# An attention layer with top-1 experts: gate and up weights as the stationary operand, row transposes ahead of up

## The chip, the cores and the metric

The kernel runs on one core of a Trainium2 chip. The metric is the device time of one execution in microseconds. Time before: 1159.86 us, the median of three runs (1158.37 to 1161.86).

## The reference

One transformer layer in fp32 on x of shape (4, 1024, 256). Causal attention with 16 heads of 16 and rotary embedding comes first, then a norm; then a feed-forward part with 8 experts, of which each token takes one:

```python
x = layernorm(x + attention(x))
xf = layernorm(x, ln_w, ln_b).reshape(-1, 256)
logits = xf @ router_w                       # 8 experts
top_idx, top_score = argmax(logits), sigmoid(max(logits))
for e in range(8):                           # gate_w, up_w: (8, 256, 512); down_w: (8, 512, 256)
    xe = xf * where(top_idx == e, top_score, 0)[:, None]
    routed += (silu(xe @ gate_w[e]) * (xe @ up_w[e])) @ down_w[e]
shared = (silu(xf @ sh_gate) * (xf @ sh_up)) @ sh_down
out = layernorm(x + (x + routed + shared))
```

## The kernel before, in words

Three programs run one after the other: `project` (queries, keys and values), `attend` (attention), and `feed` (everything behind it). Only `feed` is touched.

`feed` has two stages. In the first, 8 blocks of 512 tokens go through the output projection, two norms, the router and the shared expert. Each token's row (256 numbers, scaled by its score, and its token number behind them) is scattered by GpSimd to a table in HBM, `expert_rows`, at a place that its expert and its rank there give; the sum so far goes to `expert_sums`. Block 7, the last, runs side by side with the start of the second stage.

The second stage is one of 39 *slots* (`SLOTS`), written out, not looped by the chip. A slot j is 128 rows of one expert. Which expert it has is known at run time alone: VectorE writes it to `owner_i`, and an engine that needs it loads it into a register (`value_load`, L1027, L1038, L1046 on TensorE). A slot takes these steps:

- `load_rows(j)` on SyncE: loads the 128 rows into `rows[j % 3]`, a ring of three. `load_sums(j)` does so for the sums.
- `turn_rows(j)` on TensorE (L1020): two transposes into `front_ps`; `keep_rows(j)` on ScalarE (L1146) copies them to `rows_t`.
- `expert_gate(j)` (L1031) and `expert_up(j)` (L1041) on TensorE: two matmuls each. The rows, transposed, are the stationary operand; the weights, 512 columns at a time and addressed by the register, stream. The result has a token per partition.
- `make_silu` on ScalarE (L1133), `times_up` on VectorE (L1285): `hidden`, 128 tokens by 512.
- `turn_hidden(j)` on TensorE (L1003): four transposes; `keep_hidden(j)` on ScalarE (L1138) copies them to `hidden_t`.
- `expert_down(j)` on TensorE (L1051): four matmuls of 256 columns, into `down_ps` or, for odd slots, `front_ps`.
- `add_sum(j)` on VectorE: the sum of down's result and the loaded sum (L1367), then a CAST that takes the token numbers from the row buffer to `target_i` (L1369) and counts `targets_made`, then the moments (L1374, L1377). GpSimd makes the reciprocal deviation (L1478, L1483), VectorE's `normalise(j)` (L1382) uses it one slot later, and GpSimd scatters the result (L1491).

The order is written out by hand for each engine, and the engines meet at semaphores. TensorE's iteration j is gate(j+1), turn_hidden(j), up(j+1), turn_rows(j+2), down(j). VectorE's is times_up(j+1), normalise(j-1), add_sum(j). SyncE's is load_rows(j+3), load_sums(j+2), and for the load of rows the ring sets two waits, the rows that were in the buffer being turned and their token numbers being taken:

```python
if j >= ROW_RING:
    sp.wait_ge(rows_turned, j - ROW_RING + 1)
    sp.wait_ge(targets_made, j - ROW_RING + 1)
```

So load_rows(j+3) waits for the CAST of add_sum(j), which comes behind down(j). An fp32 matmul of the program shows as two in the trace, a transpose as one.

Of the kernel before, what the change touches and what calls it, by code (L numbers as in the profile page):

```python
# [28 lines left out]
P = 128  # L29
# [4 lines left out]
DC = D // P  # L34
# [713 lines left out]
def feed(nc, io, keep, scratch, out):  # L748
# [6 lines left out]
    with ExitStack() as ctx:  # L755
# [13 lines left out]
        row = b.sb("row", [P, 2, BT, RECORD])  # L769
        total = b.sb("total", [P, 2, BT, D])  # L770
        silu = b.sb("silu", [P, 2, INNER])
        hidden = b.sb("hidden", [P, 2, INNER])
        hidden_t = b.sb("hidden_t", [P, 2, INNER])
        shared_t = b.sb("shared_t", [P, IC, BLOCK])
        stats = b.sb("stats", [P, BT, 6])
# [79 lines left out]
        front_step = b.sem("front_step")  # L855
        gate_done, up_done, silu_made, hidden_made = (
            b.sem("gate_done"), b.sem("up_done"), b.sem("silu_made"), b.sem("hidden_made"))
        hidden_turned, hidden_t_kept, down_done, added = (
            b.sem("hidden_turned"), b.sem("hidden_t_kept"), b.sem("down_done"), b.sem("added"))
        block = ctx.enter_context(nc.Block())  # L860
        x_blocks = io["x"].rearrange("(n t p) d -> n p t d", t=BT, p=P)
        dve_stood, pool_stood = b.sem("dve_stood"), b.sem("pool_stood")
        VEC_STEPS = 16

        def slot_down(j):
            return front_ps[:, 1, :D] if j % 2 else down_ps[:]
# [61 lines left out]
        def _(pe):  # L928
# [67 lines left out]
                                            start=(c == 0), stop=(c == IC - 1))  # L996
                last.then_inc(down_done, 1)

            def turn_hidden(j):
                pe.wait_ge(hidden_made, TILES + j + 1)  # L1000
                wait(pe, hidden_t_kept, j)
                for c in range(IC):
                    last = nc.tensor.transpose(hidden_ps[:, c * P:(c + 1) * P],  # L1003
                                               hidden[:, j % 2, c * P:(c + 1) * P], ident[:])
                last.then_inc(hidden_turned, 1)

            def front_alone(n, batch, odd):
                for part in (turn_heads, times_wo, turn_xf, route, count_ranks):
                    part(n, batch, odd)
# [14 lines left out]
            def expert_gate(j):  # L1024
                if j >= SLOTS:
                    return
                e = pe.value_load(owner_i[0:1, j:j + 1], min_val=0, max_val=EXPERTS - 1)  # L1027
                pe.wait_ge(rows_t_kept, j + 1)
                pe.wait_ge(silu_made, TILES + j - 1)
                for c in range(DC):  # L1030
                    last = nc.tensor.matmul(gate_ps[:, j % 2], rows_t[:, j % 2, c * P:(c + 1) * P], gate_w[:, e, c],  # L1031
                                            start=(c == 0), stop=(c == DC - 1))
                last.then_inc(gate_done, 1)

            def expert_up(j):
                if j >= SLOTS:
                    return
                e = pe.value_load(owner_i[0:1, j:j + 1], min_val=0, max_val=EXPERTS - 1)  # L1038
                pe.wait_ge(hidden_made, TILES + j - 1)
                for c in range(DC):  # L1040
                    last = nc.tensor.matmul(up_ps[:, j % 2], rows_t[:, j % 2, c * P:(c + 1) * P], up_w[:, e, c],  # L1041
                                            start=(c == 0), stop=(c == DC - 1))
                last.then_inc(up_done, 1)

            def expert_down(j):
                e = pe.value_load(owner_i[0:1, j:j + 1], min_val=0, max_val=EXPERTS - 1)  # L1046
                pe.wait_ge(hidden_t_kept, j + 1)
                if j != 1:
                    pe.wait_ge(added, TILES + max(j - 1, 0))
                for c in range(IC):  # L1050
                    last = nc.tensor.matmul(slot_down(j), hidden_t[:, j % 2, c * P:(c + 1) * P], down_w[:, e, c],  # L1051
                                            start=(c == 0), stop=(c == IC - 1))
                last.then_inc(down_done, 1)
# [42 lines left out]
            by_batch(pe, step)  # L1096
            for j in range(SLOTS):
                expert_gate(j + 1)
                turn_hidden(j)
                expert_up(j + 1)  # L1100
                turn_rows(j + 2)
                expert_down(j)

        @block.scalar
        def _(act):
# [29 lines left out]
            def keep_hidden(j):  # L1135
                act.wait_ge(hidden_turned, j + 1)
                act.wait_ge(down_done, TILES + j - 1)
                nc.scalar.copy(hidden_t[:, j % 2], hidden_ps[:]).then_inc(hidden_t_kept, 1)  # L1138

            def keep_rows(j):  # L1140
                if j >= SLOTS:
# [6 lines left out]
            def block_step(i, odd, nxt, after):  # L1148
                def front(part):
                    if nxt is not None:  # L1150
                        part(i + 1, nxt, 1 - odd)

                for n in range(IC):
                    make_silu(i, n)
                if nxt is None:
                    keep_rows(0)
                    keep_rows(1)
                    make_silu(BLOCKS, 0)
                front(keep_xf)
# [15 lines left out]
            for j in range(SLOTS):  # L1175
                if j + 1 < SLOTS:
                    make_silu(BLOCKS, j + 1)
                keep_hidden(j)
                keep_rows(j + 2)

        @block.vector
        def _(dve):
# [93 lines left out]
            def times_up(i, t):  # L1276
                dve.wait_ge(silu_made, BT * i + t + 1)
                dve.wait_ge(up_done, BT * i + t + 1)
                if isinstance(i, int) and i == BLOCKS:
                    wait(dve, hidden_turned, t - 1)  # L1280
                    out = hidden[:, t % 2]
                else:
                    wait(dve, down_done, BT * i)
                    out = shared_t[:, t]
                nc.vector.tensor_tensor(out, silu[:, t % 2], up_ps[:, t % 2], ALU.mult).then_inc(hidden_made, 1)  # L1285

            def add_shared(i, t, odd, batch):
                dve.wait_ge(down_done, BT * i + t + 1)
                if t == 0:
                    wait(dve, sums_scattered[odd], 16 * BT * batch)  # L1290
                nc.vector.scalar_tensor_tensor(total[:, odd, t], x1[:, odd, t], 2.0, down_ps[:],
                                               ALU.mult, ALU.add).then_inc(added, 1)

            count = [0]

# [37 lines left out]
            def block_step(i, odd, batch, nxt):  # L1333
# [16 lines left out]
                add_shared(i, 3, odd, batch)  # L1350
                if nxt is None:
                    times_up(BLOCKS, 0)
                front(find_place)

            def step(batch):
                last = isinstance(batch, int) and batch == BATCH - 1
                block_step(2 * batch, 0, batch, batch)
                if last:
                    make_tables()
                block_step(2 * batch + 1, 1, batch, None if last else batch + 1)  # L1360

            def add_sum(j):
# [34 lines left out]
            for j in range(SLOTS):  # L1397
                if j + 1 < SLOTS:
                    times_up(BLOCKS, j + 1)
                if j >= 1:  # L1400
                    normalise(j - 1)
                add_sum(j)
            normalise(SLOTS - 1)

# [161 lines left out]
```

## Time and profile before

| | |
|---|---|
| three runs, median (range) | 1159.86 us (1158.37 to 1161.86) |
| profiled execution, own time | 1158.47 us |
| its span, first to last instruction | 1156.8 us |
| TensorE matmul busy | 1037.1 us (90%) |
| VectorE busy | 700.3 us (61%) |
| ScalarE busy | 459.7 us (40%) |
| GpSimd busy | 337.2 us (29%) |
| mean granted TensorE clock | 0.944 of full |

`project` ends near 94 us, `attend` near 626 us, the blocks near 899 us; the slots take the rest. The busy time counts work, not the engine's speed at it, and "PE busy" holds pipelined matmuls whose ends are modelled: the distance of two starts tells more than the length of one. PE is TensorE's matmuls, PEld its weight loads, DVE is VectorE, ACT ScalarE, POOL GpSimd, SPq SyncE's queue.

### The profile page before, as it was taken

The page shows a single profiled execution, that of the slowest core. Times are in us where ns is not written, and L with a number is a line of the kernel's source. Part 1 is how long each engine was busy: PE and PEld are TensorE (multiplying, and loading weights), DVE is VectorE, ACT ScalarE, POOL GpSimd, SP SyncE. Part 2 cuts the span into 40 slices and gives each one's busy share as a digit, 9 for nine tenths or more (in the row PEclk, how much of TensorE's full clock was granted, in tenths as well). Part 3 has the DMA queues.
Part 4 walks back from the last instruction along what each step waited for, and adds up shares of the span by engine and source line. Part 5 has one row for each costly group of instructions (what it writes and reads, how often), then busy time and mean ns, then how long its engine had stood idle before and what let it go on. Part 6 is the DMA issues. An engine that isn't in the chain of part 4 may idle for free. (4 is left out here: it accounts for less than half of the span.)

```text
span 1156.8 us, 17516 instructions
## 1 busy us (share of the span) xinstructions
PE 1037.1 (90%) x5522; PEld 541.2 (47%) x5522; DVE 700.3 (61%) x1708; ACT 459.7 (40%) x687; POOL 337.2 (29%) x480
## 2 busy tenths in 40 slices
PE   8991799999999999999982799999994999999995
PEld 4550234444444444444322566666652555555553
DVE  4994688888888888888702455555550233333332
ACT  2442046666666666666670222222220222222221
POOL 2334312222222222222212123333346232222222
PEclk9996579999999999999996699999996999999998
DMA  7557534455554554554009212222112121222121
GB/s 277 140 137 165 80 62 65 68 109 93 88 109 73 102 101 66 102 103 66 11 10 285 57 56 74 75 75 74 38 53 102 56 65 62 67 62 68 61 66 37
DMA packets 78277, 100.06 MB, mean 87 GB/s; under 512 B 28048, under 2 KB 64400, under 8 KB 74864
## 3 DMA queue, kind: packets, MB, share of 16 engines
q1 hardware_dynamic: 67568, 74.41, 31.2%
q0 software_dynamic: 5712, 15.93, 3.7%
q10 hardware_dynamic: 4912, 8.66, 2.3%
q8 instruction: 45, 0.74, 0.3%
q14 instruction: 40, 0.33, 0.1%
HBM read 65.86 MB, written 32.70 MB: 85 GB/s over the span
## 5 line engine op out<-in xcount | busy, mean ns | idle before, releaser
L572 ACT ACTIVATE probs<-scores_ps 128x1024 f32<-128x1024 f32 (+3 forms) x384 | 290.3, 809 | 133.2 <-PE scores_ps L505 131.7
L632 DVE TENSOR_REDUCE maxima<-max_ps 128x1 f32<-128x512 f32 (+2 forms) x352 | 231.6, 687 | 53.0 <-PE max_ps L485 29.2
L481 PE MATMUL max_ps<-k_stack,q_stack 96*128 96x512 bf16 (+3 forms) x768 | 232.9, 345 | 33.5 <-DMA q_stack<-q_parts 32.5
L505 PE MATMUL scores_ps<-q_stack,k_stack 99*128 99x512 bf16 (+3 forms) x768 | 183.0, 328 | 2.2 <-ACT probs L572 2.0
L722 POOL TENSOR_SCALAR_AFFINE_SELECT probs<-probs 128x512 f32<-128x512 f32 x128 | 81.2, 634 | 333.1 <-ACT probs L572 332.2
L525 PE MATMUL out_ps<-probs,v_ones 128*32 128x512 f32 (+3 forms) x1536 | 164.3, 499 | 2.6 <-POOL probs L722 1.8
L481 PEld LDWEIGHTS max_ps<-k_stack,q_stack 96*128 96x128 bf16 x768 | 75.8, 99 | 192.4 <-DVE maxima L628 59.0
L628 DVE CUSTOM_DVE_ANT_0 masked_out<-max_ps,mask_wide 128x384 bf16<-128x384 f32 (+1 forms) x256 | 151.3, 622 | 19.0 <-PE max_ps L481 16.4
L1133 ACT ACTIVATE silu<-gate_ps 128x512 f32<-128x512 f32 x71 | 42.4, 597 | 236.7 <-PE gate_ps L1031 140.0
L505 PEld LDWEIGHTS scores_ps<-q_stack,k_stack 99*128 99x128 bf16 x768 | 69.4, 99 | 53.2 <-ACT probs L572 11.8
L1285 DVE TENSOR_TENSOR hidden<-silu,up_ps 128x512 f32<-128x512 f32 x39 | 26.8, 688 | 104.9 <-PE up_ps L1041 104.9
L995 PE MATMUL down_ps<-sh_down_sb,shared_t 128*128 128x256 f32 x256 | 65.1, 400 | 21.1 <-issue 13.9
L1491 POOL DMA_INDIRECT out<-final,target_i x39 | 42.4, 1088 | 112.8 <-DVE final L1382 109.0
L1031 PE MATMUL gate_ps<-gate_sb,rows_t 128*128 x156 | 73.4, 593 | 0.7 <-ACT rows_t L1146 0.7
L1041 PE MATMUL up_ps<-up_sb,rows_t 128*128 x156 | 73.4, 593 | 0.0
L1441 POOL DMA_INDIRECT expert_rows<-row,place_i x32 | 31.1, 972 | 118.3 <-DVE place_i L1270 93.1
L995 PEld LDWEIGHTS down_ps<-sh_down_sb,shared_t 128*128 128x128 f32 x256 | 49.0, 199 | 34.8 <-issue 19.0
L161 PE MATMUL qk_ps<-x_t,w_qk 128*128 128x512 f32 x128 | 59.7, 610 | 5.5 <-DMA w_qk<-in_Wq 5.5
L980 PE MATMUL gate_ps<-xf_t,sh_gate_sb 128*128 128x512 f32 x128 | 60.2, 593 | 0.0
L987 PE MATMUL up_ps<-xf_t,sh_up_sb 128*128 128x512 f32 x128 | 60.1, 592 | 0.0
L525 PEld LDWEIGHTS out_ps<-probs,v_ones 128*32 128x32 f32 x1536 | 30.7, 108 | 58.6 <-issue 44.5
L259 POOL TENSOR_TENSOR rest<-rot,parts 128x1024 f32<-128x1024 f32 x16 | 34.0, 2126 | 66.3 <-ACT parts L193 62.9
(150 smaller groups left out, 1264.2 us busy)
## 6 DMA issues: line engine op xcount, KB each, us to landing
k_stack<-k_parts SPq DMA_DIRECT2D x96, 128.0 KB, 4.5
q_stack<-q_parts SPq DMA_DIRECT2D x96, 128.0 KB, 7.5
q_parts<-parts SPq DMA_DIRECT2D x32, 192.0 KB, 3.2
k_parts<-parts SPq DMA_DIRECT2D x32, 192.0 KB, 3.0
rows_in<-expert_rows SPq DMA_DIRECT2D x39, 136.0 KB
sums_in<-expert_sums SPq DMA_DIRECT2D x39, 128.0 KB, 2.0
x_t<-in_x_cols SPq DMA_DIRECT2D x8, 512.0 KB, 10.9
heads_rows<-heads_out SPq DMA_DIRECT2D x32, 128.0 KB, 1.7
```

What stands on the lines that cost most here:

```text
L481: last = nc.tensor.matmul(part, q_stack[:ROWS, u.slot, h0 + k, t * P:(t + 1) * P], k_stack[:ROWS, u.slot, h0 + k, chunk * BLOCK:chunk * BL ...
L505: last = nc.tensor.matmul(scores_ps[:, pair, k, n0:], k_stack[:ROWS_MAX, u.slot, h, mt * P:(mt + 1) * P], q_stack[:ROWS_MAX, u.slot, h, c ...
L525: last = nc.tensor.matmul(out_ps[32 * h:32 * h + 32, n0:], v_ones[:, u.slot, mt, h], probs[:, s % RING, h, n0:], start=(mt == 0), stop=las ...
L572: nc.scalar.activation(probs[:, s % RING, 2 * pair:2 * pair + 2, n0:], scores_ps[:, pair, :, n0:], ACT.Exp).then_inc(exp_done, 1)
L628: nc.vector.tensor_tensor_reduce(masked_out[:, n % 6, :keys], bank("piece", u.i, n)[:, :keys], mask_wide[:, BLOCK - keys:], 1.0, NEG, ALU. ...
L632: nc.vector.tensor_reduce(maxima[:, u.slot, chunk, h0:h0 + heads, t], bank("piece", u.i, n)[:, :heads * keys].rearrange("p (h k) -> p h k" ...
L722: nc.gpsimd.affine_select(out=tile, in_=tile, compare_op=ALU.is_ge, fill=0.0, base=0, pattern=[[0, GROUP], [1, P]], channel_multiplier=-1) ...
L980: last = nc.tensor.matmul(gate_ps[:, n % 2], sh_gate[:, c, n * P:(n + 1) * P], xf_t[:, odd, c], start=(c == 0), stop=(c == DC - 1))
L987: last = nc.tensor.matmul(up_ps[:, n % 2], sh_up[:, c, n * P:(n + 1) * P], xf_t[:, odd, c], start=(c == 0), stop=(c == DC - 1))
L995: last = nc.tensor.matmul(down_ps[:], shared_t[:, c, t * P:(t + 1) * P], sh_down[:, c], start=(c == 0), stop=(c == IC - 1))
L1031: last = nc.tensor.matmul(gate_ps[:, j % 2], rows_t[:, j % 2, c * P:(c + 1) * P], gate_w[:, e, c], start=(c == 0), stop=(c == DC - 1))
L1041: last = nc.tensor.matmul(up_ps[:, j % 2], rows_t[:, j % 2, c * P:(c + 1) * P], up_w[:, e, c], start=(c == 0), stop=(c == DC - 1))
```

## The change

Gate and up of a slot are computed in the transposed form: the weights are the stationary operand, 128 columns at a time, and the transposed rows stream. The result comes out with the inner index on the partitions, as down needs it, so `turn_hidden`, `keep_hidden` and the tile `hidden` go, and `times_up` writes `hidden_t` itself. The register no longer addresses the weights on TensorE. Instead each slot's gate weights (1024 numbers per partition) are copied two slots ahead by ScalarE (`copy_gate`) into `gate_now`, which takes the space of `heads`, and the up weights by VectorE (`copy_up`) into `up_now`, in the space of `res`; both are double buffers. `turn_rows(j + 2)` is now ahead of `expert_up(j + 1)`. SyncE's and GpSimd's parts are as before.

```diff
+        gate_copied, up_copied, act_stood = b.sem("gate_copied"), b.sem("up_copied"), b.sem("act_stood")
+
+        gate_now = heads[:].rearrange("p o t g e -> p o (t g e)").rearrange("p o (c n) -> p o c n", c=DC)
+        up_now = res[:].rearrange("p o t d -> p o (t d)").rearrange("p o (c n) -> p o c n", c=DC)
...
             def expert_gate(j):
                 if j >= SLOTS:
                     return
-                e = pe.value_load(owner_i[0:1, j:j + 1], min_val=0, max_val=EXPERTS - 1)
                 pe.wait_ge(rows_t_kept, j + 1)
                 pe.wait_ge(silu_made, TILES + j - 1)
-                for c in range(DC):
-                    last = nc.tensor.matmul(gate_ps[:, j % 2], rows_t[:, j % 2, c * P:(c + 1) * P], gate_w[:, e, c],
-                                            start=(c == 0), stop=(c == DC - 1))
+                pe.wait_ge(gate_copied, j + 1)
+                for n in range(IC):
+                    for c in range(DC):
+                        last = nc.tensor.matmul(gate_ps[:, j % 2, n * P:(n + 1) * P],
+                                                gate_now[:, j % 2, c, n * P:(n + 1) * P],
+                                                rows_t[:, j % 2, c * P:(c + 1) * P],
+                                                start=(c == 0), stop=(c == DC - 1))
                 last.then_inc(gate_done, 1)
...
             def expert_down(j):
                 e = pe.value_load(owner_i[0:1, j:j + 1], min_val=0, max_val=EXPERTS - 1)
-                pe.wait_ge(hidden_t_kept, j + 1)
+                pe.wait_ge(hidden_made, TILES + j + 1)
...
             for j in range(SLOTS):
                 expert_gate(j + 1)
-                turn_hidden(j)
+                turn_rows(j + 2)
                 expert_up(j + 1)
-                turn_rows(j + 2)
                 expert_down(j)
...
+            def copy_gate(j):
+
+                if j >= SLOTS:
+                    return
+                e = act.value_load(owner_i[0:1, j:j + 1], min_val=0, max_val=EXPERTS - 1)
+                if j >= 2:
+                    act.wait_ge(gate_done, TILES + j - 1)
+                stand(act, act_stood)
+                nc.scalar.copy(gate_now[:, j % 2], gate_w[:, e]).then_inc(gate_copied, 1)
...
                 if j + 1 < SLOTS:
                     make_silu(BLOCKS, j + 1)
-                keep_hidden(j)
                 keep_rows(j + 2)
+                copy_gate(j + 2)
...
+            def copy_up(j):
+
+                if j >= SLOTS:
+                    return
+                e = dve.value_load(owner_i[0:1, j:j + 1], min_val=0, max_val=EXPERTS - 1)
+                if j >= 2:
+                    dve.wait_ge(up_done, TILES + j - 1)
+                stand(dve, dve_stood)
+                nc.vector.tensor_copy(up_now[:, j % 2], up_w[:, e]).then_inc(up_copied, 1)
...
                 if j >= 1:
                     normalise(j - 1)
+                copy_up(j + 2)
                 add_sum(j)
```

`expert_up` changes as `expert_gate` does. The copies for slots 0 and 1 are made in block 7: ScalarE's copy_gate(0) after the block's four silu, copy_gate(1) after slot 0's silu; VectorE's copy_up(0) after `make_tables`, ahead of block 7's step, and copy_up(1) at that step's end.

TensorE's program for one slot in the slots' stage, before; `rows_in` are the loaded rows, `rows_t` the transposed ones, `v_then_down` the down weights:

```order
L1027 TENSOR_LOAD owner_i
L1027 ISA x2
L1031 ISA [waits silu_made,rows_t_kept]
L1031 MATMUL gate_ps<-gate_sb,rows_t 128x512
L1031 ISA
L1031 MATMUL gate_ps<-gate_sb,rows_t 128x512
L1003 MATMUL hidden_ps<-ident,hidden 128x128 [waits hidden_t_kept,hidden_made]
L1003 MATMUL hidden_ps<-ident,hidden 128x128 x3
L1038 TENSOR_LOAD owner_i
```

It goes on with up's two matmuls (L1041), the row transposes (L1020, which wait for rows_in) and down (L1051). And now, where `heads_in` is the space of `gate_now` and `res` that of `up_now`:

```order
L1027 MATMUL gate_ps<-rows_t,heads_in 128x128 [waits gate_copied,silu_made,rows_t_kept]
L1027 MATMUL gate_ps<-rows_t,heads_in 128x128 x7
L1015 MATMUL front_ps<-ident,rows_in 128x128 [waits rows_t_kept,rows_in2]
L1015 MATMUL front_ps<-ident,rows_in 128x128
L1040 MATMUL up_ps<-rows_t,res 128x128 [waits up_copied,hidden_made]
L1040 MATMUL up_ps<-rows_t,res 128x128 x7
L1047 TENSOR_LOAD owner_i
```

The wait for the loaded rows has moved from behind up to behind gate, and nothing but gate stands between down of the slot before and it. VectorE's program of a slot, now:

```order
L1295 TENSOR_TENSOR hidden_t<-silu,up_ps 128x512 [waits down_done,up_done,silu_made]
L1406 TENSOR_SCALAR final<-final,slot_moments,slot_rstd 128x256 [waits slot_moments_made,slot_rstd_made]
L1308 TENSOR_LOAD owner_i
L1308 ISA x2
L1312 ISA [waits up_done]
L1312 COPY res<-up_sb 128x1024
L1391 TENSOR_TENSOR final<-front_ps,sums_in 128x256 [waits out_stored1,sums_in2,down_done]
L1393 CAST target_i<-rows_in 128x1
```

The four rows of L1308 and L1312 are new; before, the sum (there L1367) followed the scale (there L1382) at once.

## Rows read from the trace of the kernel before

**Rows 1.** The page, part 2: TensorE's granted clock in 40 slices

```profile
PEclk9996579999999999999996699999996999999998
```

**Rows 2.** Timeline of one slot: start us, us, engine, line, what, [idle before]

```profile
1001.90 1.88 PE L1031 MATMUL gate_ps<-gate_sb,rows_t 128*128 x4
1002.11 0.42 DVE L1367 TENSOR_TENSOR final<-front_ps,sums_in 128x256 f32<-128x256 f32 x1 [1.33 <-PE front_ps L1051]
...
1002.45 0.14 DVE L1369 CAST target_i<-rows_in 128x1 int32<-128x1 f32 x1
...
1003.49 0.33 SPq L900 DMA_DIRECT2D rows_in<-expert_rows  x1
1003.62 0.60 PE L1003 MATMUL hidden_ps<-ident,hidden 128*128 128x128 f32 x4
...
1004.06 1.88 PE L1041 MATMUL up_ps<-up_sb,rows_t 128*128 x4
...
1005.68 0.24 PEld L1020 LDWEIGHTS front_ps<-ident,rows_in 128*128 128x128 f32 x2 [0.57 <-DMA rows_in<-expert_rows]
...
1006.03 0.69 DVE L1285 TENSOR_TENSOR hidden<-silu,up_ps 128x512 f32<-128x512 f32 x1 [2.70 <-PE up_ps L1041]
...
1006.57 1.99 PE L1051 MATMUL down_ps<-v_then_down,hidden_t 128*128 x8 [0.41 <-issue]
1006.64 0.41 DVE L1382 TENSOR_SCALAR final<-final,slot_moments,slot_rstd 128x256 f32<-128x256 f32 x1
...
1008.40 1.88 PE L1031 MATMUL gate_ps<-gate_sb,rows_t 128*128 x4
1008.60 0.42 DVE L1367 TENSOR_TENSOR final<-down_ps,sums_in 128x256 f32<-128x256 f32 x1 [1.55 <-PE down_ps L1051]
```

**Rows 3.** Waits, 905 to 1140 us: total us, times, longest

```profile
PEld front_ps L1020 <- DMA rows_in<-expert_rows: 16.5, 36, 0.9
```

**Rows 4.** SyncE's queue: its waits in that stretch, and its register load in rows 2

```profile
SPq L898 <- DVE target_i L1369: 144.4, 36, 4.3
...
L899 SPq TENSOR_LOAD <-source_i x1: 375/375/375, 1002.7 to 1002.7; - x1
```

**Rows 5.** Timeline: add_sum of slot 0, the next rows' load, add_sum of slot 36

```profile
906.91 0.42 DVE L1367 TENSOR_TENSOR final<-down_ps,sums_in 128x256 f32<-128x256 f32 x1 [1.19 <-PE down_ps L1051]
...
910.27 0.14 PEld L1020 LDWEIGHTS front_ps<-ident,rows_in 128*128 128x128 f32 x1 [0.35 <-DMA rows_in<-expert_rows]
...
1136.07 0.42 DVE L1367 TENSOR_TENSOR final<-down_ps,sums_in 128x256 f32<-128x256 f32 x1 [1.39 <-PE down_ps L1051]
```

**Rows 6.** Timeline of a block: transposes, down, the router, the next transposes

```profile
820.03 1.04 PE L952 MATMUL front_ps<-ident,xf 128*128 128x128 f32 x8
...
820.90 1.89 PE L995 MATMUL down_ps<-sh_down_sb,shared_t 128*128 128x256 f32 x8
...
822.42 1.97 PEld L961 LDWEIGHTS hidden_ps<-router_sb,xf_t 128*128 128x128 f32 x16
...
824.23 0.94 PEld L934 LDWEIGHTS front_ps<-ident,heads_in 128*128 128x128 f32 x8
```

**Rows 7.** Groups by form: line, engine, what | busy us, mean ns | idle before

```profile
L1204 DVE TENSOR_TENSOR res<-front_ps,res 128x1024 f32<-128x1024 f32 x8 | 9.8, 1225 | 27.2 <-issue 16.7 <-PE front_ps L943 10.5
...
L1118 ACT COPY xf_t<-front_ps 128x1024 f32<-128x1024 f32 x8 | 8.1, 1012 | 68.2 <-PE front_ps L952 68.2
```

**Rows 8.** ScalarE's timeline: the first keep_rows

```profile
893.98 0.37 ACT L1146 COPY rows_t<-front_ps 128x256 f32<-128x256 f32 x1 [25.72 <-remote]
```

**Rows 9.** Windows: busy us of PE, PEld, DVE, ACT, POOL; PEclk; DMA share; GB/s

```profile
600.00:605.00 5.00, 4.29 (x30) 0.78 (x28) 0.00 (x0) 3.38 (x4) 0.00 (x0) 1.00 0.00 0
871.00:874.00 3.00, 0.07 (x1) 0.00 (x0) 0.42 (x1) 0.00 (x0) 2.37 (x3) 0.86 0.28 106
```

**Rows 10.** TensorE's timeline behind that pause: down of block 7

```profile
874.01 3.78 PE L995 MATMUL down_ps<-sh_down_sb,shared_t 128*128 128x256 f32 x8 [2.94 <-issue]
```

More of the change, by code:

```diff
@@ L771, in feed @@
         silu = b.sb("silu", [P, 2, INNER])
-        hidden = b.sb("hidden", [P, 2, INNER])
         hidden_t = b.sb("hidden_t", [P, 2, INNER])
@@ L857, in feed @@
             b.sem("gate_done"), b.sem("up_done"), b.sem("silu_made"), b.sem("hidden_made"))
-        hidden_turned, hidden_t_kept, down_done, added = (
-            b.sem("hidden_turned"), b.sem("hidden_t_kept"), b.sem("down_done"), b.sem("added"))
+        down_done, added = b.sem("down_done"), b.sem("added")
         block = ctx.enter_context(nc.Block())
@@ L997, in down @@
                 last.then_inc(down_done, 1)
[L999 to L1005, printed above, removed]
             def front_alone(n, batch, odd):
@@ L1037, in expert_up @@
                     return
-                e = pe.value_load(owner_i[0:1, j:j + 1], min_val=0, max_val=EXPERTS - 1)
                 pe.wait_ge(hidden_made, TILES + j - 1)
-                for c in range(DC):
-                    last = nc.tensor.matmul(up_ps[:, j % 2], rows_t[:, j % 2, c * P:(c + 1) * P], up_w[:, e, c],
-                                            start=(c == 0), stop=(c == DC - 1))
+                pe.wait_ge(up_copied, j + 1)
+                for n in range(IC):
+                    for c in range(DC):
+                        last = nc.tensor.matmul(up_ps[:, j % 2, n * P:(n + 1) * P],
+                                                up_now[:, j % 2, c, n * P:(n + 1) * P],
+                                                rows_t[:, j % 2, c * P:(c + 1) * P],
+                                                start=(c == 0), stop=(c == DC - 1))
                 last.then_inc(up_done, 1)
@@ L1133, in make_silu @@
                 nc.scalar.activation(silu[:, t % 2], gate_ps[:, t % 2], ACT.Silu).then_inc(silu_made, 1)
[L1135 to L1138, printed above, removed]
+            def copy_gate(j):
[6 more added lines that the diff above has]
+                nc.scalar.copy(gate_now[:, j % 2], gate_w[:, e]).then_inc(gate_copied, 1)
             def keep_rows(j):
@@ L1155, in block_step @@
                 if nxt is None:
+                    act.wait_ge(tables_made, 1)
+                    act.wait_ge(heads_turned, BLOCKS)
+                    act.wait_ge(keep["weights_in"], 16 * 2 * EXPERTS)
+                    copy_gate(0)
                     keep_rows(0)
@@ L1158, in block_step @@
                     make_silu(BLOCKS, 0)
+                    copy_gate(1)
                 front(keep_xf)
@@ L1279, in times_up @@
                 if isinstance(i, int) and i == BLOCKS:
-                    wait(dve, hidden_turned, t - 1)
-                    out = hidden[:, t % 2]
+                    dve.wait_ge(down_done, TILES + t - 1)
+                    out = hidden_t[:, t % 2]
                 else:
@@ L1352, in block_step @@
                     times_up(BLOCKS, 0)
+                    copy_up(1)
                 front(find_place)
@@ L1359, in step @@
                     make_tables()
+                    dve.wait_ge(tables_made, 1)
+                    dve.wait_ge(keep["weights_in"], 16 * 2 * EXPERTS)
+                    copy_up(0)
                 block_step(2 * batch + 1, 1, batch, None if last else batch + 1)
```

## The prediction

> **What bounds the kernel now.** I read the page first, then the stage that the change touches. The profiled execution takes 1158.47 us at a span of 1156.8 us; the median of the three runs is 1159.86 us, 1.4 us above it, and a measurement of this kernel can tell about 0.3% (3.5 us) from no change. TensorE is busy 90% of the span, and its granted clock is full in the slots' stage (the last nine digits of PEclk) [rows 1]. So the natural reading is that TensorE's own work is the bound there. The timeline of one slot tells more [rows 2]. Array starts follow each other without a hole from gate (1001.90) over the transposes of hidden (1003.62) to up (1004.06). Then TensorE stands: the weight load of the row transposes at 1005.68 waited 0.57 us for the DMA into rows_in, and 36 slots have such a wait, 0.46 us each [rows 3]. So the row load is already the last to arrive, by a little.
>
> Where does that load start? Within rows 2: add_sum(j) begins 0.21 us after the last matmul of down(j) ends (1002.11 against the next start, 1001.90); its CAST of the row numbers, at 1002.45, ends at 1002.59; SyncE has waited for that CAST in all 36 slots [rows 4], then loads a register in 0.375 us, works out the address and issues the DMA at 1003.49. The transposes can start at 1005.68, 3.57 us after add_sum began. From there it is 2.92 us to the next add_sum (1008.60). The mean over 36 slots, from the first and the 37th add_sum, is (1136.07 - 906.91) / 36 = 6.37 us [rows 5]. With the 2.9 us behind the load, which is TensorE's work, the mean from add_sum to transposes is 3.47 us.
>
> **The change part by part.** *The row transposes move ahead.* They take rows j+3 in the iteration that follows down(j), which is just when the load of rows j+3 is started, by add_sum(j). SyncE's program is untouched, and so is the ring of three. Before, gate, the transposes of hidden and up stood between down(j) and that wait: 1.72 + 0.44 + 1.72 = 3.88 us of cover [rows 2]. After, gate alone does. So TensorE finishes gate 1.5 us after add_sum(j) began and then stands until 3.47 us: 1.9 us in place of 0.46. This is the heart of the forecast. Behind the wait, in TensorE's order, are up(j+2) and down(j+1), and down(j+1) is what add_sum(j+1) needs, so a ring closes: add_sum, load, row transposes, up, down, add_sum. Nothing queued in it can be done early.
>
> *The ring's length.* 3.47 us to the transposes; 0.22 for two of them (0.44 for four, rows 2) and about 0.1 until the array is in up; up; down, 1.72 us (the 1.83 us from 1006.57 to 1008.40, less the 0.11 us of a first weight load that nothing hid); 0.2 to add_sum.
>
> *Up and gate in the transposed form.* Each was 2 matmuls of 512 columns in the program and 4 in the array, 1.72 us. Now it is 8 of 128 columns, 16 in the array, and each needs a weight load. The columns streamed are the same: down passes 256 columns in 1.83/8, about 0.22 us [rows 2], so 128 take 0.11. The loads' price is seen where matmuls are shortest: the router's, 8 columns wide, are 16 loads from 822.42 to 824.23, 0.113 us a pair [rows 6]. The transposes, 128 columns wide, are 8 from 820.03 to 820.90, 0.109 us a pair. Both sides being about 0.11, 16 pairs take 1.72 to 1.81 us if load and stream overlap; I take 1.76. If they did not, each pair would cost 0.22 and the part 3.4 us; that is a rival below. Down speaks for overlap: a pair of its takes 0.22 us, though it holds a load with the router's price, 0.11, and a stream of 0.21.
>
> The ring is then 3.47 + 0.32 + 1.76 + 1.72 + 0.2 = 7.47 us, against 6.37: +1.10 us, times 36 slots = **+39.6 us**. The 0.44 us of removed transposes, the ScalarE copy of hidden and the two address loads of gate and up are gone from TensorE and ScalarE, and are worth nothing inside this ring.
>
> *VectorE's copy of up* stands between normalise and add_sum, in the ring. VectorE starts times_up 0.25 us after up ends (1006.03 against 1005.78) and has finished normalise at 1007.05, 1.27 us after up's end [rows 2]; add_sum could start 1.72 + 0.2 = 1.92 us after it. So 0.65 us are free. No 1024-wide SBUF copy on VectorE is in the trace. Above, the nearest row is the 1024-wide sum, 1225 ns [rows 7]; below, the 256-wide scale, 0.41 us [rows 2]. At 1.22 us add_sum is 0.57 us late in each slot, at 0.65 or less not at all. The 1024-wide row is the nearest in size, but it reads two tensors, one in PSUM; I take 0.9 us, between the ends, so 0.25 us late, 36 x 0.25 = **+9 us**, and keep 0 and +21 us for the range. The register load ahead of it (0.375 us on SyncE) can run while times_up and normalise do. The Trainium skill (VectorE: DVE Perf Modes, "What auto-detection actually checks") says that a one-source op with source and destination in SBUF takes a two-port mode, which would halve the copy; an estimate by it is 0.65 us (half of the 1225 ns, and a little for the start), and by that the term of 9 us would be near 0. No row here shows it.
>
> *ScalarE's copy of gate*: 1.01 us, as its 1024-wide copies have now [rows 7]. It follows keep_rows, which ends about 0.8 us after the row transposes start; the copy ends near 1.9 us, while gate(j+2) comes at 0.32 + 1.76 + 1.72 = 3.8 us. Hidden by up and down; without that cover it would cost up to 1 us a slot. times_up (0.69 us) now feeds down directly, but down(j+1) comes a whole gate, wait and up after times_up(j+1) could start: hidden.
>
> *The ends.* copy_up(0) goes into VectorE's program ahead of the last block: up to +1 us. The first slot loses 0.44 us of transposes. In the last two slots no rows are loaded; there add_sum, moments, GpSimd's rstd and normalise form a chain that is as long as before: -0.4. Together about 0. The stretch between the blocks and the slots holds waits that nothing in the program explains: ScalarE's first keep_rows stands 25.72 us behind a "remote" releaser [rows 8]. Programs of another length may shift it; I allow 5 us to both sides.
>
> Sum: 1158.5 + 39.6 + 9 + 0 = **1207 us**, about 4% slower.
>
> **The rivals.**
> *The load hides (faster).* If rows_in landed by gate's end, 1.5 us after add_sum began, TensorE would be the bound: gate 1.76, transposes 0.22, up 1.76, down 1.72, about 0.1 of issue, 5.56 us a slot, 0.8 less, 36 x 0.8 = 29 us: 1129 us. It decides below 1.5 us from add_sum to transposes, and between 1.5 and 2.4 us the kernel still gains. For it speaks only that TensorE's work shrinks by 0.44 us a slot; against it, that SyncE's issue alone comes 1.38 us after add_sum [rows 2]. Chance 5%.
>
> *Weight loads do not overlap.* Gate at 3.4 us still fits under the row wait; up adds 1.7 us, 36 x 1.7 = 61: 1268 us. The Trainium skill (TensorE: Matmul & The Clock Gate, "The mechanism") says that a weight load overlaps running matmuls only where its row group differs, and all loads here take the whole array. By that rule the time is this rival's. Down's 0.22 us a pair disagrees with the rule. Chance 6%.
>
> *The clock falls.* TensorE would stand 1.9 us in 7.5. The granted clock stayed full at 4.29 us busy in 5 [rows 9], and fell within a pause from 871 to 874 (0.86 on average), after which eight of down's matmuls took 3.78 us [rows 10] in place of 1.8 to 2.0 [rows 2, 6]. No pause of 1.9 us is in the trace. At the lower level of 1.2 GHz gate, transposes, up and down double: 3.47 + 0.5 + 3.5 + 3.45 + 0.2 = 11.1 us a slot, +131 us more: 1338 us. Chance 4%.
>
> *The change does not reach the ring* (the copies or the transposed form leave the time where it is): 2%.
>
> **How the numbers follow.** The forecast has 83%. Its own ends: ring at 1.72 for up and a load of 3.36 us (910.27 - 906.91, the first of rows 5), no delay by VectorE, gives 36 x 0.95 = +34: 1192; a delay of 0.57 and up at 1.81 gives 36 x 1.72 = +62, and some of the 5 us: 1224. The range is 1192 to 1224; beyond it lie the rivals, 17%. Slower by over 0.3%: 83 + 6 + 4 = 93%; faster 5%; within 0.3% 2%.
>
> **What would show it.** The wait of the row transposes for rows_in should be near 1.9 us in 36 slots, at full clock; the interval of add_sum 7.4 to 7.9 us; gate and up 1.7 to 1.8 us each; SyncE's wait on the CAST still there. A VectorE COPY of 0.65 us would put the time near 1198. I am wrong if rows_in has landed when gate ends, if weight loads are 0.2 us apart, or if PEclk leaves 1.0.

## The result, and the profile after

The changed kernel takes 1203.76 us, the median of four runs (1201.37 to 1205.09), against 1159.36 us for the kernel before in the same session: ratio 1.0377, 95% interval 1.0354 to 1.0401. It is slower by 3.8%. The forecast was 1207 us, range 1192 to 1224. The profiled execution took 1201.37 us at a span of 1199.6 us, 42.8 us more than before.

The page of the changed kernel, the span, engines' busy time, granted clock and the chain that ended last:

```profile
span 1199.6 us, 19075 instructions
...
PE 1024.9 (85%) x6302; PEld 610.9 (51%) x6302; DVE 725.8 (61%) x1747; ACT 481.9 (40%) x687; POOL 345.9 (29%) x480
...
PEclk9996589999999999999975999999969999999998
...
PE 31%; DMA 7%; issue 4%; DVE 3%; SPq 2%; another core or an unknown queue 1%; POOL 0%; DVEq 0%; ACT 0%; POOLq 0%
DMA rows_in<-expert_rows 6%; PE up_ps L1040 6%; PE up_ps L990 5%; PE gate_ps L983 5%; PE down_ps L998 4%; PE down_ps L1052 3%; PE front_ps L1052 2%; PE front_ps L946 2%; PE front_ps L1015 1%; SPq L902 1%; PE hidden_ps L964 1%; DVE xf L1239 1%; PE front_ps L955 1%; PE front_ps L937 1%
```

TensorE did 12 us less work than before (1037.1 us then) in a span 43 us longer, and the load of the rows, which the chain of the kernel before holds once in the slots' stage (2.11 us at 1092.86), is now its largest single entry. One slot of the changed kernel in the timeline, to be held against [rows 2]; L1015 is turn_rows, L1040 up, L1052 down, L1027 gate, L1391 the sum and L1393 the CAST of add_sum:

```profile
1001.71 0.20 PEld L1015 LDWEIGHTS front_ps<-ident,rows_in 128*128 128x128 f32 x2 [1.79 <-DMA rows_in<-expert_rows]
...
1001.99 1.95 PE L1040 MATMUL up_ps<-rows_t,res 128*128 128x128 f32 x16
1002.19 0.37 ACT L1151 COPY rows_t<-front_ps 128x256 f32<-128x256 f32 x1 [1.44 <-PE front_ps L1015]
1002.89 1.05 ACT L1143 COPY heads_in<-gate_sb 128x1024 f32 x1 [0.34 <-issue]
...
1003.77 1.89 PE L1052 MATMUL front_ps<-v_then_down,hidden_t 128*128 x8
1004.03 0.69 DVE L1295 TENSOR_TENSOR hidden_t<-silu,up_ps 128x512 f32<-128x512 f32 x1 [4.43 <-PE up_ps L1040]
1004.63 0.41 DVE L1406 TENSOR_SCALAR final<-final,slot_moments,slot_rstd 128x256 f32<-128x256 f32 x1
1005.01 0.69 DVE L1312 COPY res<-up_sb 128x1024 f32 x1
...
1005.50 1.95 PE L1027 MATMUL gate_ps<-rows_t,heads_in 128*128 128x128 f32 x16
1005.70 0.42 DVE L1391 TENSOR_TENSOR final<-front_ps,sums_in 128x256 f32<-128x256 f32 x1
1006.04 0.14 DVE L1393 CAST target_i<-rows_in 128x1 int32<-128x1 f32 x1
...
1006.99 0.33 SPq L903 DMA_DIRECT2D rows_in<-expert_rows  x1
```

Up starts 0.28 us after the row transposes, down 1.78 us later, gate 1.73 us after that, add_sum 0.20 us into gate. SyncE issues the next load 1.29 us after add_sum starts. Gate is over at 1007.3; the transposes of the next rows must wait. The waits of 912 to 1185 us, where [rows 3] has 16.5 us:

```profile
PEld front_ps L1015 <- DMA rows_in<-expert_rows: 68.7, 36, 2.3
```

68.7 us over 36 slots are 1.91 us each. This is idle time of the weight loads, as in [rows 3]; the matmul array stands a little less, 61.8 us or 1.72 us each. The first add_sum and the one of slot 36, and the row transposes behind the first:

```profile
909.14 0.42 DVE L1391 TENSOR_TENSOR final<-down_ps,sums_in 128x256 f32<-128x256 f32 x1
...
912.53 0.20 PEld L1015 LDWEIGHTS front_ps<-ident,rows_in 128*128 128x128 f32 x2 [1.84 <-DMA rows_in<-expert_rows]
...
1179.17 0.42 DVE L1391 TENSOR_TENSOR final<-down_ps,sums_in 128x256 f32<-128x256 f32 x1
```

The mean slot is (1179.17 - 909.14) / 36 = 7.50 us against 6.37 [rows 5]; the median interval is 7.42 us. So the slots cost 36 x 7.50 - 36 x 6.37 = 40.9 us more (from the unrounded times); the first add_sum comes 2.2 us later in the span than before, and the tail behind the 37th is 0.3 us shorter. Together that is the 42.8 us.

### The profile page after: what moved, and what is told of

Its sections match the earlier page's. It is cut to its first block and busy times, and to the rows that moved or that the text cites. A ratio compares the mean times of both kernels' runs of the same rounds, so it can differ in the third digit from the quotient of the medians.

```text
span 1199.6 us, 19075 instructions
## 1 busy us (share of the span) xinstructions
PE 1024.9 (85%) x6302; PEld 610.9 (51%) x6302; DVE 725.8 (61%) x1747; ACT 481.9 (40%) x687; POOL 345.9 (29%) x480
## 5 line engine op out<-in xcount | busy, mean ns | idle before, releaser
L1295 DVE TENSOR_TENSOR hidden_t<-silu,up_ps 128x512 f32<-128x512 f32 x39 | 26.8, 688 | 170.6 <-PE up_ps L1040 170.6
L1516 POOL DMA_INDIRECT out<-final,target_i x39 | 50.2, 1288 | 179.4 <-DVE final L1406 173.8
L1040 PE MATMUL up_ps<-rows_t,res 128*128 128x128 f32 x624 | 77.7, 279 | 0.0
L1027 PEld LDWEIGHTS gate_ps<-rows_t,heads_in 128*128 128x128 f32 x624 | 76.1, 193 | 1.9
L1027 PE MATMUL gate_ps<-rows_t,heads_in 128*128 128x128 f32 x624 | 76.4, 276 | 0.0
L1040 PEld LDWEIGHTS up_ps<-rows_t,res 128*128 128x128 f32 x624 | 74.4, 195 | 0.1
L1015 PE MATMUL front_ps<-ident,rows_in 128*128 128x128 f32 x78 | 17.4, 306 | 61.8 <-DMA rows_in<-expert_rows 61.8
```

The source lines that it names most:

```text
L1027: last = nc.tensor.matmul(gate_ps[:, j % 2, n * P:(n + 1) * P], gate_now[:, j % 2, c, n * P:(n + 1) * P], rows_t[:, j % 2, c * P:(c + 1) * P],
L1040: last = nc.tensor.matmul(up_ps[:, j % 2, n * P:(n + 1) * P], up_now[:, j % 2, c, n * P:(n + 1) * P], rows_t[:, j % 2, c * P:(c + 1) * P], ...
```

## The experiments

Each ratio is to the kernel before, run in turns on the same chip. That kernel took 1151 us on one of the chips used and 1159 us on another, so times of different groups are compared by ratio only. A "slot" below is the median interval of two add_sum in a profile; before, it is 6.33 us (mean 6.37).

### The form alone, and the move alone

`form_alone` is the changed kernel with the old place of the row transposes, `move_alone` the kernel before with the new one.

```diff
 form_alone (against the changed kernel); move_alone is the reverse, against the kernel before
                 expert_gate(j + 1)
-                turn_rows(j + 2)
                 expert_up(j + 1)
+                turn_rows(j + 2)
                 expert_down(j)
```

> The changed kernel with turn_rows(j+2) put back behind expert_up(j+1): the transposed form and the copies without the move. Theory of the row-load ring (SyncE may load rows j+3 only after the CAST of add_sum(j)): the ring is 3.41 us from add_sum to the transposes, about 0.9 us to down (the register load of down is again stuck behind the wait), 1.83 us of down and 0.2 us: 6.3 us a slot, as in the kernel before (6.37), so 1158 to 1162 us, although TensorE has 0.44 us less to do per slot. Rival, TensorE-bound reading (90% busy): the transposes that went are worth 0.44 us a slot, 1141 to 1145 us. Rival, the form costs (weight loads, copies): 1195 us or more, as in the changed kernel.

Measured: 1151.41 us against 1151.08, ratio 1.0003 (0.9994 to 1.0013), slot 6.34 us. TensorE has the 0.44 us of transposes less to do in each slot (gate and up take 0.13 us of it back), and the time does not move. The ring theory holds and both rivals fall. (Its forecast in microseconds, 1158 to 1162, was for a chip on which the kernel before takes 1159; here it took 1151.) Where the 0.44 us went is in the timeline of this kernel, and in the rows of TensorE's register load for down (L1047):

```profile
1001.11 0.42 DVE L1391 TENSOR_TENSOR final<-down_ps,sums_in 128x256 f32<-128x256 f32 x1 [0.78 <-PE down_ps L1052]
...
1004.45 0.20 PEld L1015 LDWEIGHTS front_ps<-ident,rows_in 128*128 128x128 f32 x2
...
1005.31 1.99 PE L1052 MATMUL front_ps<-v_then_down,hidden_t 128*128 x8 [0.42 <-issue]
...
1007.34 0.42 DVE L1391 TENSOR_TENSOR final<-front_ps,sums_in 128x256 f32<-128x256 f32 x1 [0.93 <-PE front_ps L1052]
```

```profile
L1047 PEldq TENSOR_LOAD <-owner_i x1: 304/304/304, 1004.5 to 1004.5; - x1
L1047 PEldq FUSED_REGOPS  x1: 151/151/151, 1004.8 to 1004.8; - x1
```

The transposes start 3.34 us after the add_sum at 1001.11 and the next add_sum comes 2.89 us later; in [rows 2] it was 3.57 and 2.92. The array does not stand ahead of the transposes here. It stands ahead of down: the register load of down comes behind the wait for the rows in TensorE's program, so it starts only at 1004.5, with the transposes, and down comes behind it at 1005.31. So the ring runs over the load of the rows and this register load to down, whatever TensorE's work beside it is. In the median of the 36 slots down starts 4.30 us after add_sum, against 4.31 in the kernel before.

> The kernel before with turn_rows(j+2) in front of expert_up(j+1), nothing else: gate, transposes of hidden, row transposes, up, down. Ring theory: the wait for rows_in grows from 0.46 to about 1.4 us, the ring is 3.41 + 0.3 + 1.72 + 1.72 + 0.2 = 7.35 to 7.45 us a slot, +36 us: 1192 to 1198 us. Rival, the slowdown comes from the form (weight loads or copies) and not from the place of the row transposes: 1158 to 1163 us.

Measured: 1213.25 us, ratio 1.0538 (1.0491 to 1.0585), slot 7.90 us, mean 8.20. So the place of the transposes slows the old form too, and by more than I expected. Two things were missing from my sum. First, the old up needs a register load on TensorE (0.30 us, and 0.15 for the address, L1038), and that now stands behind the wait:

```profile
999.72 0.20 PEld L1020 LDWEIGHTS front_ps<-ident,rows_in 128*128 128x128 f32 x2 [1.45 <-DMA rows_in<-expert_rows]
999.73 0.44 PE L1020 MATMUL front_ps<-ident,rows_in 128*128 128x128 f32 x2 [1.21 <-DMA rows_in<-expert_rows]
...
1000.57 0.69 PE L1041 MATMUL up_ps<-up_sb,rows_t 128*128 x1 [0.41 <-issue]
```

Up starts 0.84 us behind the transposes, in place of 0.28 in the changed kernel, whose up has no such load; the median is 0.75, so 0.5 us a slot. Second, the granted clock fell in five slots, each 1.7 to 2.2 us longer; the first slot, 1.4 us longer, began at the lower clock. The windows around one of them (us, then busy time of PE, PEld, DVE, ACT, POOL, then PEclk):

```profile
1023.00:1025.00 2.00, 1.18 (x4) 0.71 (x5) 0.00 (x0) 0.37 (x1) 0.00 (x0) 0.97 0.22 67
1025.00:1027.00 2.00, 2.00 (x3) 0.72 (x3) 0.00 (x0) 0.00 (x0) 0.00 (x0) 0.50 0.00 0
1027.00:1029.00 2.00, 2.00 (x7) 1.48 (x6) 1.01 (x2) 0.00 (x0) 0.14 (x1) 0.68 0.03 8
1029.00:1031.00 2.00, 2.00 (x8) 1.12 (x7) 1.07 (x4) 0.00 (x0) 0.95 (x1) 1.00 0.16 66
```

### A fourth row buffer

```diff
 ring4_after (against the changed kernel), ring4_before (against the kernel before)
-    ROW_RING, SUM_RING, CONSTS, RANKS = 3, 3, 14, P
+    ROW_RING, SUM_RING, CONSTS, RANKS = 4, 3, 14, P
```

> The changed kernel with a ring of four row buffers in place of three, so that the load of rows j+4 waits for add_sum(j) and each load has a slot more. Ring theory: no wait for rows_in, TensorE's work bounds the slot: 1.79 (gate) + 0.22 + 1.79 (up) + 1.73 = 5.5 to 5.6 us, 36 x 1.95 = 70 us less than the changed kernel: 1130 to 1136 us. Rival, the load's own 2 us or SyncE's chain sets the pace whatever the ring: 1195 us or more. Rival, another chain (VectorE's add_sum, GpSimd's rstd, the scatter of the result) is next at 6 us or more: 1150 us or more.

Measured: 1118.32 us, ratio 0.9711 (0.9695 to 0.9727), slot 5.52 us. From 3.8% slower to 2.9% faster by one number (the two ratios are from different chips). In the window from 912 to 1095 us TensorE is never idle by the record, at full clock, and no wait for rows_in is left. The window, then TensorE's timeline of one slot:

```profile
912.00:1095.00 183.00, 183.00 (x1392) 176.22 (x1391) 91.18 (x234) 62.89 (x99) 69.33 (x100) 1.00 0.25 74
```

```profile
1001.28 1.95 PE L1027 MATMUL gate_ps<-rows_t,heads_in 128*128 128x128 f32 x16
1003.06 0.38 PE L1015 MATMUL front_ps<-ident,rows_in 128*128 128x128 f32 x2
1003.28 1.95 PE L1040 MATMUL up_ps<-rows_t,res 128*128 128x128 f32 x16
1005.07 1.89 PE L1052 MATMUL down_ps<-v_then_down,hidden_t 128*128 x8
```

Gate takes 1.78 us, the transposes 0.22, up 1.79, down 1.73: 5.52 us, and it is TensorE's work alone.

> The kernel before with a ring of four row buffers. Ring theory: its wait of 0.46 us a slot goes, and with it part of the gap ahead of down, since the register load can be done during up: 1.72 + 0.44 + 1.72 + 0.22 + 1.73 = 5.83 to 5.9 us a slot in place of 6.37, 1139 to 1143 us. Rival, the wait only moves (another chain is right behind): 1155 us or more.

Measured: 1125.84 us, ratio 0.9776 (0.976 to 0.9793), slot 5.82 us. The kernel before was in the same ring, 0.5 us deep. Without it the new form is worth its 0.3 us a slot (0.44 us of transposes, less 0.14 us that gate and up take longer). Both kernels with four buffers came out some 0.4 to 0.5% below what I had expected (1139 to 1143 us of 1159 is a ratio of 0.982 to 0.986 for this one, 1130 to 1136 one of 0.975 to 0.980 for ring4_after). A part of it is that the first slots are shorter still, 2.58 and 4.17 us here; the rest was not taken apart.

### When the CAST is made

Four buffers loosen the ring, but do not show which step of it matters. Two kernels move the CAST of the token numbers, which counts `targets_made`, in the changed kernel with three buffers.

```diff
 early_cast (late_cast puts the same two lines behind bn_aggr, at the end of add_sum)
+            def take_targets(j):
+                if j >= 2:
+                    dve.wait_ge(out_stored[j % 2], 16 * (j // 2))
+                nc.vector.tensor_copy(target_i[:, j % 2:j % 2 + 1],
+                                      rows[:, j % ROW_RING, D:D + 1]).then_inc(targets_made, 1)
+
             def add_sum(j):
...
-                nc.vector.tensor_copy(target_i[:, j % 2:j % 2 + 1],
-                                      rows[:, j % ROW_RING, D:D + 1]).then_inc(targets_made, 1)
...
             for j in range(SLOTS):
+                dve.wait_ge(rows_t_kept, j + 1)
+                take_targets(j)
                 if j + 1 < SLOTS:
                     times_up(BLOCKS, j + 1)
```

> The changed kernel once more, unedited, beside the kernels of this group. Ratio to the kernel before 1.035 to 1.041, add_sum intervals of 7.4 us; the granted clock falls in one or a few slots, as in its first profile (one) and in that of the move alone (five).

Measured: 1202.41 us against 1159.65, ratio 1.0373 (1.0355 to 1.039), slot 7.40 us; one slot at the lower clock, as in the first profile.

> The changed kernel, ring of three, with the CAST of the row numbers taken out of add_sum(j) and put at the head of VectorE's iteration j, ahead of times_up(j+1). If it is this CAST behind down(j) that starts the load late, the load now starts some 3 us earlier and has landed when gate ends: slots of 5.5 us, as with four buffers, ratio to before 0.968 to 0.975. If the buffers' number itself or the load's time is what counts, the ratio stays at 1.03 or more.

Measured: 1128.67 us, ratio 0.9735 (0.9719 to 0.9751), slot 5.52 us. Three buffers are enough if the numbers are taken early. It was the 144-ns CAST behind down(j) that started the load late. The mean slot is 5.59 us, since the CAST now waits for the scatter of two slots ago to land, and in a few slots this wait makes add_sum late (at 1086.57 it was 2.73 us, and that slot 6.47 us long):

```profile
1001.90 0.15 DVE L1389 CAST target_i<-rows_in 128x1 int32<-128x1 f32 x1 [1.64 <-DMA out<-final,target_i]
...
1002.86 0.33 SPq L903 DMA_DIRECT2D rows_in<-expert_rows  x1
```

> The changed kernel with the same CAST put behind the moments, at the end of add_sum(j), 0.75 us later. Ring theory: every slot longer by that, 8.15 us in place of 7.4, 36 x 0.75 = 27 us more than the changed kernel: ratio to before 1.060 to 1.066 if the clock holds. TensorE then stands about 2.6 us in each slot, and if such pauses make the granted clock fall in some slots, more slots show it than in the changed kernel and the ratio is above 1.066. Rival, the CAST is not in the ring: no change, 1.038.

Measured: 1276.24 us, ratio 1.1008 (1.099 to 1.1027). Six slots of the 36 took 8.1 to 8.5 us, as the ring theory says for the full clock; the other 30 took about 9.9 us. The expectation for a falling clock was the direction alone; 30 slots of 1.8 us more are some 53 us, about twice the 27 us expected for the CAST. A slot of the long kind, in windows:

```profile
1008.00:1009.00 1.00, 0.00 (x0) 0.00 (x0) 0.00 (x0) 0.00 (x0) 0.00 (x0) 1.00 0.48 133
1009.00:1010.00 1.00, 0.94 (x8) 0.94 (x9) 0.00 (x0) 0.37 (x1) 0.00 (x0) 1.00 0.40 131
1010.00:1012.00 2.00, 2.00 (x12) 2.00 (x11) 0.00 (x0) 1.04 (x1) 0.00 (x0) 0.54 0.00 0
1012.00:1014.00 2.00, 2.00 (x7) 1.68 (x7) 1.67 (x3) 0.00 (x0) 0.39 (x1) 0.61 0.00 0
1014.00:1016.00 2.00, 2.00 (x18) 1.92 (x17) 1.07 (x4) 0.00 (x0) 0.93 (x1) 1.00 0.16 66
```

TensorE stood 2.41 us before the transposes at 1009.06, and about 1 us after it had begun to work again the clock went to the lower level, for some 3 us.

### The copies

```diff
 no_copies
             def copy_gate(j):
-                if j >= SLOTS:
+                if j >= 2:
                     return
...
-                pe.wait_ge(gate_copied, j + 1)
+                pe.wait_ge(gate_copied, min(j, 1) + 1)
```

and the same for `copy_up`.

> The changed kernel without copy_gate and copy_up for slots 2 to 38: the weights of slots 0 and 1 are used for all, so the experts' part is computed with other weights. Ring theory: VectorE's copy of 0.69 us ends just before add_sum can start and ScalarE's is hidden, so the time stays: ratio to before 1.034 to 1.041. Rival, the copies are part of the loss: up to 36 x 0.69 = 25 us less, ratio 1.016. The prediction's term for VectorE's copy, 9 us, would give 1.030.

Measured: 1199.11 us, ratio 1.0344 (1.0327 to 1.0361), slot 7.41 us against 7.40 with the copies. The median slot does not change. The 3.3 us between the two medians (1199.11 and 1202.41, and no run of one kernel lies among those of the other) are for the most part inside the mean slot, 7.42 against 7.49 us: 1.6 us of it is the one slot at the lower clock, which this profile does not have, and 0.8 us are three slots (the 1st, 16th and 31st) of 7.6 to 7.7 us, in which VectorE stood 0.3 us ahead of its copy. VectorE's copy, from the groups by form of the changed kernel's slots, and one of those three slots in its timeline:

```profile
L1312 DVE COPY res<-up_sb 128x1024 f32 x36 | 25.0, 694 | 0.9 <-issue 0.9
```

```profile
1027.68 0.70 DVE L1312 COPY res<-up_sb 128x1024 f32 x1 [0.32 <-issue]
1028.30 0.41 DVE L1391 TENSOR_TENSOR final<-down_ps,sums_in 128x256 f32<-128x256 f32 x1
```

It ends at 1005.70 in the timeline above, and add_sum starts at 1005.70, 0.20 us after gate, as before. It is hidden to within a few hundredths, with nothing to spare: in the three slots add_sum starts 0.48 us after gate.

### What the move is for

With the ring gone, the place of the transposes can be judged by itself.

> The kernel before with four row buffers and the row transposes in front of up: the move alone, where the ring of three is gone. Ring theory: no wait for rows_in whatever the place, slots of 5.8 to 5.9 us as with four buffers and no move, ratio to before 0.975 to 0.982. Rival, the place costs by itself (rows_t or register loads late): 0.99 or more.

Measured: 1126.73 us, ratio 0.9788 (0.9772 to 0.9804), slot 5.82 us, as expected: in the old form the place is worth nothing.

> The changed kernel with four row buffers and the row transposes back behind up: the form alone, without the ring. Ring theory: 5.52 us a slot, the same as with the transposes in front, ratio to before 0.968 to 0.975. If the place has a worth of its own (ScalarE's keep_rows and copy_gate earlier), this one is slower than that by over 0.3%.

Measured: 1133.23 us, ratio 0.9843 (0.9827 to 0.9859), slot 5.96 us. That is 1.4% slower than with the transposes in front, and against the first expectation. In the new form the place has a worth:

```profile
1004.60 0.38 PE L1015 MATMUL front_ps<-ident,rows_in 128*128 128x128 f32 x2
...
1005.02 0.37 ACT L1151 COPY rows_t<-front_ps 128x256 f32<-128x256 f32 x1 [1.41 <-PE front_ps L1015]
...
1005.72 1.05 ACT L1143 COPY heads_in<-gate_sb 128x1024 f32 x1 [0.33 <-issue]
...
1006.91 2.02 PE L1027 MATMUL gate_ps<-rows_t,heads_in 128*128 128x128 f32 x16 [0.20 <-ACT heads_in L1143]
```

ScalarE copies the gate weights after it has kept the rows, so gate(j+2) waits for transposes, keep_rows, a register load and 1.05 us of copy; down's 1.73 us do not cover that. In front of up they have 1.79 us more.

> The changed kernel with four row buffers and copy_up(0) moved in VectorE's program from behind the tables to behind the fourth times_up of block 7. In the changed kernel TensorE stood 1.4 us for the first times_up of that block. If that pause is on the path, 1 to 1.5 us less than with four buffers alone (ratio 0.970 against 0.971); if the waits of the stretch up to the first slot swallow it, no change. A difference this small may not show.

```diff
 ring4_late_copy (against ring4_after)
                 times_up(i, 3)
+                if nxt is None:
+                    dve.wait_ge(tables_made, 1)
+                    dve.wait_ge(keep["weights_in"], 16 * 2 * EXPERTS)
+                    copy_up(0)
                 front(shift_second)
```

with the same three lines taken out behind `make_tables`. Measured: 1116.88 us, ratio 0.9696 (0.968 to 0.9712). Against 0.9711 the intervals overlap: no difference that these runs can tell. It is the lowest ratio of all, and both it and ring4_after beat both kernels of this case.

## Why the prediction was right, point by point

*The ring* was the cause. The prediction said that the row transposes would stand where the load of their rows has only just begun, for 1.9 us in each of 36 slots; they stood 1.91 us. Undoing the move takes the loss away (form_alone, 1.0003), the move alone brings it to the old form (1.0538), a fourth buffer or an earlier CAST removes it with the move in place (0.9711, 0.9735), and a later CAST makes it grow (1.1008).

*One reading of the kernel before* was wrong. The prediction has TensorE stand ahead of the row transposes, 0.46 us in each slot. That is idle time of the weight loads; the array goes from up to the transposes without a hole, as gate's start at 1001.90 and 3.88 us of work give just this start:

```profile
1005.78 0.38 PE L1020 MATMUL front_ps<-ident,rows_in 128*128 128x128 f32 x2
```

The hole is behind them, ahead of down (1006.57, where 1006.00 was possible), and it is down's register load, held up by the wait for the rows. (With four buffers down follows the start of the transposes after 0.22 us, in place of 0.64.) So the 2.9 us behind the load are not all TensorE's work, and the ring was closed before, as the prediction says, but over this register load, which the prediction does not name. Its 3.47 us from add_sum to the transposes was a remainder, 6.37 - 2.9, and not a row; in the kernel before the array starts them 3.67 us after add_sum in the median. That it came within 0.05 us of the changed kernel's 3.42 is in part luck.

*The ring's length* was 7.47 us by the sum, and 7.42 us by the median slot. Its parts: from add_sum to the transposes 3.42 us in the median and 3.39 in the first slot (3.47 expected), transposes to up 0.28 (0.32), up 1.78 (1.76), down 1.73 (1.72), to add_sum 0.20. The mean is 7.50 us. The difference over 36 slots, some 2.9 us, is 1.6 us for one slot at the lower clock (8.99 us), 0.8 us for the three slots with the late copy, and 0.7 us for two slots more: in one (7.84 us) the rows took 2.57 us from SyncE's issue to the transposes in place of 2.13, in the other (7.71 us) SyncE issued 0.35 us later.

*Gate and up in the new form* took 0.11 us for each load and matmul together, as taken. The rival of weight loads that do not overlap is refuted: 16 pairs of it would last 3.4 us, and up lasts 1.79. The Trainium skill's rule (TensorE: Matmul & The Clock Gate, "The mechanism"), by which a load overlaps only where its row group differs, does not hold for these loads of the whole array. The same section also lets a load run ahead when it goes to the background weight buffer, and that is what the rows look like.

*VectorE's copy* was the term that was mis-sized: I took 0.9 us and +9 us, it is 0.69 us and costs nothing in the median slot; both copies together, with all that goes with them, are worth 3.3 us (no_copies). The 1225-ns row was a poor neighbour. The Trainium skill's rule of a two-port mode for such a copy (VectorE: DVE Perf Modes, "What auto-detection actually checks"), from which I had estimated 0.65 us, agrees with the trace's 0.69 us. That the total came out near all the same is luck in this part: other small terms went the other way, the clock (1.6 us), the longer slots, and 2.2 us up to the first add_sum for which I had about nothing. Without the 9 us the forecast would have been 1198.1 us, 3.3 us below the profiled execution and 5.7 below the median; with them it was 5.7 us above the one and 3.3 above the other.

*ScalarE's copy* (1045 ns, 1.01 taken) is hidden as argued, but only by the move: with four buffers ring4_behind shows it on the path as soon as up no longer follows the transposes.

*The clock* was given 4% as an event of every slot. It fell in one slot of 36, here in windows of that slot, where TensorE began again at 1143.99:

```profile
1143.00:1144.00 1.00, 0.01 (x1) 0.01 (x1) 0.00 (x0) 0.00 (x0) 0.00 (x0) 1.00 0.35 113
...
1145.00:1146.00 1.00, 1.00 (x7) 1.00 (x6) 0.00 (x0) 0.82 (x1) 0.00 (x0) 0.50 0.00 0
```

The rival was not far off: the array pauses for about 1.7 us of 7.4 in the changed kernel and one slot is lost, for 2.4 us and more of 8.2 in late_cast and 30 are. Why just this one slot of the changed kernel fell is not shown. Its pause was 1.90 us, and four slots with 1.95 to 2.10 us kept the full clock; it was the same slot in both profiles of this kernel.

*The words on the removed work* were right for this ring only: the new form, with the transposes of hidden and two register loads gone, is worth 0.3 us a slot when the ring is gone, and the register load of up alone is worth 0.5 us a slot when the transposes stand in front of it (move_alone). I had not priced that, and so expected a ratio of about 1.03 where 1.054 was measured.

What stays open: why VectorE stands 0.3 us ahead of its copy in three slots, in the same three in both profiles of the changed kernel, and how far the pauses of block 7 shift with the length of the programs. The 2.2 us to the first add_sum were not taken apart.

## What to carry to other kernels

Before moving a consumer of a load earlier, find the instruction that frees its buffer and see what lies between the two: here a small CAST at the end of a slot started the load, and the busy share (90%) had hidden that the loop was already tied to it. If a wait for a DMA closes a loop over several engines, a further buffer, or reading the last value out of the old buffer as early as possible, can be worth more than work taken off the busiest engine: here 2.2 to 2.9% against nothing. And a pause in each turn can cost more than its own length, once the clock follows it.

## What the runs showed of the hardware that was not expected

- GpSimd's scatter of the results takes 1288 ns on average in the changed kernel and 1089 ns without the copies, the groups by form of the two kernels, the changed one first:

```profile
L1516 POOL DMA_INDIRECT out<-final,target_i x39 | 50.2, 1288 | 179.4 <-DVE final L1406 173.8 <-issue 5.5
```

```profile
L1516 POOL DMA_INDIRECT out<-final,target_i x39 | 42.5, 1089 | 177.8 <-DVE final L1406 172.2 <-issue 5.6
```

  In the timeline the scatter starts 0.3 us into VectorE's copy. In the trace of the changed kernel 35 of the 39 scatters overlap a copy of VectorE's and take 1311 ns on average, the other four 1086 ns, and none overlaps a copy of ScalarE's. So it goes with VectorE's copy; a kernel with that copy alone was not run. It costs nothing here.
- The fall of the clock is not in proportion to the pause. With about 1.7 us of pause in a slot of 7.4 one slot in 36 fell to the 1.2 GHz level, with 2.4 us and more in 8.2 it was 30. In the old form with the move, with a pause of 1.2 to 1.4 us ahead of the transposes and another of 0.3 to 0.4 us ahead of up, it was five.
- The stretch between the blocks and the first slot differs with the chip: where the kernel before took 1159 us, VectorE's sums of block 7 stood 15.1 us behind a "remote" releaser in its profile, and where it took 1151 us no such wait shows in the profiles of the other kernels there. What the releaser is was not found.
